# A new layout of steps in a fused two-layer Perceiver, with the context's low parts formed by POOL

## The reference, cut to what matters

```python
def _L0_xattn_ref(q, k, v, Wq, Wk, Wv, Wo):      # q = layernorm(x), k = v = ctx_1024
    qh = _split_heads(q @ Wq.T)                   # 16 heads of 16
    kh = _split_heads(k @ Wk.T)
    vh = _split_heads(v @ Wv.T)
    scores = jnp.einsum('bhqd,bhkd->bhqk', qh, kh) * scale
    attn = jax.nn.softmax(scores, axis=-1)
    out = jnp.einsum('bhqk,bhkd->bhqd', attn, vh)
    ...
    return out @ Wo.T
...
x = x + _L0_xattn_ref(_layernorm(x, axis=-1), ctx_1024, ctx_1024, ...)
x = x + _L0_attn_ref(...)     # a small attention over heads
x = x + _L0_ffn_ref(...)      # one expert of 8, picked by the largest gate
x = x + _L1_xattn_ref(...)    # as layer 0, with biases
x = x + _L1_attn_ref(...)     # a linear recurrence, gelu and a norm
x = x + _L1_ffn_ref(...)      # two of 8 experts for gate, up and down
```

## Time and profile before

| what | value |
|---|---|
| median of 3 runs | 1105.58 us (1102.05 to 1106.64) |
| the profiled execution's own time | 1103.75 us |
| its span | 1101.9 us |
| PE busy | 968.3 us (88%) |
| DVE, ACT busy | 635.1 us (58%), 557.4 us (51%) |
| POOL busy | 150.6 us (14%) |
| granted TensorE clock, mean | 0.954 of full |

### The profile page before, as it was taken

The page is one execution under the profiler, slowest core; times in us unless marked ns, Lnnn a source line. Parts: engine busy times, 40 slices in busy tenths (PEclk is TensorE's granted clock), DMA queues, the critical chain, the costliest instruction groups (busy, mean ns, idle before and its releaser), DMA issues.

```text
span 1101.9 us, 34691 instructions
## 1 busy us (share of the span) xinstructions
PE 968.3 (88%) x15092; PEld 617.5 (56%) x15092; DVE 635.1 (58%) x1063; ACT 557.4 (51%) x1028; POOL 150.6 (14%) x182
## 2 busy tenths in 40 slices
PE   4778789998989999899898898896558999999998
PEld 2455456655655665565565565665345444445887
DVE  5655655656565566666657657665457454446342
ACT  4466757565676665457456565655147212122210
POOL 4211112111111211112111121110000000000000
PEclk9989899999999999999999999998559999999999
DMA  7686465452634443343434424341101232322210
GB/s 264 185 288 192 109 203 139 115 174 70 184 101 121 106 122 86 109 104 107 109 104 117 116 73 115 86 137 42 63 1 39 77 111 81 113 79 97 96 39 20
DMA packets 70461, 123.72 MB, mean 112 GB/s; under 512 B 34420, under 2 KB 45716, under 8 KB 67048
## 3 DMA queue, kind: packets, MB, share of 16 engines
q1 hardware_dynamic: 69480, 119.84, 36.8%
q0 software_dynamic: 544, 1.34, 0.3%
q10 hardware_dynamic: 288, 0.33, 0.1%
HBM read 64.81 MB, written 17.31 MB: 75 GB/s over the span
## 4 chain that ended last, share of the span: by engine, by line
PE 67%; DVE 12%; ACT 6%; SPq 6%; issue 4%; DMA 4%; POOL 0%; ACTq 0%; DVEq 0%
PE ps L595 65%; SPq L379 6%; DVE mpart L1185 4%; ACT p L966 2%; PE ps L844 2%; DMA stage<-in_wkv 1%; DMA c32b<-in_ctxT 1%; DVE rinv L1202 1%; PE ps L730 1%; ACT ch L924 1%; DMA cl<-cparts 1%; ACT kh L941 1%; ACT k L940 1%; DMA qbscratch<-qb 1%; ACT wh L977 1%
## 5 line engine op out<-in xcount | busy, mean ns | idle before, releaser
L1185 DVE TENSOR_REDUCE mpart<-ps 128x2 f32<-128x800 f32 (+1 forms) x256 | 252.9, 990 | 132.8 <-PE ps L595 132.5
L966 ACT ACTIVATE p<-ps 128x512 f32<-128x512 f32 (+1 forms) x416 | 225.7, 600 | 80.3 <-PE ps L595 80.0
L547 POOL TENSOR_TENSOR kl<-k,kh 128x400 f16<-128x400 f32 (+1 forms) x128 | 118.9, 930 | 496.8 <-ACT kh L941 496.6
L595 PE MATMUL ps<-p,v 128*17 128x64 f32 x6656 | 138.5, 226 | 6.5 <-DVE osum L1212 6.5
L595 PE MATMUL ps<-kh,qbcur 64*128 64x400 f16 (+1 forms) x512 | 87.9, 340 | 53.9 <-DVE mpart L1185 49.6
L595 PEld LDWEIGHTS ps<-p,v 128*17 128x17 f32 x6656 | 101.9, 100 | 47.7 <-issue 32.4
L1216 DVE SCALAR_TENSOR_TENSOR wl<-w,wh 128x2048 f16<-128x2048 f32 x24 | 55.0, 2292 | 127.3 <-ACT wh L977 127.3
L595 PE MATMUL ps<-wvh,ch 128*128 128x256 f16 (+1 forms) x416 | 114.9, 276 | 0.9 <-issue 0.2
L595 PE MATMUL ps<-wvh,cl 128*128 128x256 f16 (+1 forms) x416 | 113.8, 274 | 0.4 <-issue 0.4
L595 PE MATMUL ps<-wvl,ch 128*128 128x256 f16 (+1 forms) x416 | 113.8, 274 | 0.0
L977 ACT ACTIVATE wh<-w 128x2048 f16<-128x2048 f32 x24 | 45.8, 1909 | 112.6 <-PE ps L595 112.6
(11 more groups left out here) (206 smaller groups left out, 1386.2 us busy)
## 6 DMA issues: line engine op xcount, KB each, us to landing
ks<-kh SPq DMA_DIRECT2D x256, 100.1 KB
w<-in_wgu SPq DMA_DIRECT2D x16, 1024.0 KB, 4.8
ks<-kl SPq DMA_DIRECT2D x128, 100.1 KB
w<-in_wd SPq DMA_DIRECT2D x8, 1024.0 KB, 4.7
c32a<-in_ctxT SPq DMA_DIRECT2D x16, 400.5 KB, 4.2
cparts<-ch SPq DMA_DIRECT2D x8, 800.5 KB, 6.6
cparts<-cl SPq DMA_DIRECT2D x8, 800.5 KB, 8.4
c32a<-in_ctxT SPq DMA_DIRECT2D x12, 400.0 KB, 3.2
```

Source lines behind the costliest of these rows:

```text
L547: nc.gpsimd.tensor_tensor(kl[:, mt, k0:k0 + w], k32[:, ku % 2, 0:w], kh[:, mt, k0:k0 + w], ALU.subtract).then_inc(sem("klo_done"), 1)
L595: return nc.tensor.matmul(o, lhsT, rhs, start=start, stop=stop, skip_group_check=shared)
L966: nc.scalar.activation(p32[0:n, step % PRING, BANK * side:BANK * side + BANK], ps[0:n, side, :], ACT.Exp, scale=DH ** -0.5).then_inc(sem(" ...
L1185: nc.vector.reduce_max(mpart[:, j0:j0 + 3:2, quarter], o.rearrange("p (b c) -> p b c", b=2)[:, :, 0:w], AX.X).then_inc(sem("max_done"), 1)
```

## The change

The table of units is written anew; two more tables say which tiles each `W` weighs and which units lie in the second PSUM slot. No step now has two `P` units without a `K` or `V` unit between them, the weighting is two steps behind the scores (tiles 0 and 1 both in step 3), `O` stands at the end of step 4, and `divide` half 1 at the end of step 5, `take_sums` in step 2. ACT makes the exponentials before it copies out a `K`, `N` or `V` unit that stands right before `S` (`scores_first`). In the rounds POOL forms `cl` (`ctx_low`) after the step's `kl`, where DVE did. Three stages move to other steps.

```diff
 STEP_UNITS = {0: ["V2", "S", "P0", "W"],
-              1: ["P1", "V3", "S", "P2", "W"],
...
+              4: ["K4", "S", "P5", "W", "O"],
+              5: ["V6", "P6", "K5", "S", "P7", "W"],
+              6: ["K6", "S", "P8", "W"],
...
+              10: ["N1", "S", "P13", "W"],
+              11: ["N2", "S", "P14", "W"],
+              12: ["S", "P15", "N3", "W", "T"]}
+
+WEIGH_AT = {0: (11,), 1: (12,), 3: (0, 1), **{k: (k - 2,) for k in range(4, KT)}}
+SUMS_STEP, DIVIDE_STEP = 2, 5
+
+SECOND_BANK = ("V3", "V5", "K4", "K5", "K7", "V1", "N1", "N3")
 CTX_STEPS = {4: 0, 6: 1, 8: 2, 10: 3}
-LAG = 3
...
-STAGE_AT = {(0, 4): 1, (0, 5): 2, (0, 7): 3, (0, 9): 4, (0, 12): 5, (1, 4): 6, (1, 10): 7}
+STAGE_AT = {(0, 3): 1, (0, 5): 2, (0, 7): 3, (0, 9): 4, (0, 12): 5, (1, 7): 6, (1, 12): 7}
...
+def scores_first(units):
+
+    at = units.index("S")
+    if at and units[at - 1][0] in "KNV":
+        return units[:at - 1] + ["S", units[at - 1]] + units[at + 1:]
+    return units
...
+            def ctx_low(n):
+                h, kc, u, at = n % 4 // 2, n % 2, n // 4 % 2, ctx_slot(n)
+                k0, w = HALVES[h]
+                pool.wait_ge(sem("chi_done"), n + 1)
+                nc.gpsimd.tensor_tensor(cl[u][:, kc, k0:k0 + w], c32[at][:, 0:w], ch[u][:, kc, k0:k0 + w],
+                                        ALU.subtract).then_inc(sem("clo_done"), 1)
...
                         if name[0] in "KN" and has_unit(name, g):
                             klo(round_of(name, g), int(name[1]))
+                    if k in CTX_STEPS and g + 2 < B:
+                        ctx_low(4 * (g + 2) + CTX_STEPS[k])
...
-                    for name in STEP_UNITS[k]:
+                    for name in scores_first(STEP_UNITS[k]):
                         if name == "S":
                             exps(g, k)
...
                         if name == "S":
-                            if k == LAG and g:
+                            if k == SUMS_STEP and g:
                                 take_sums(g - 1)
-                            if k == LAG + 2 and g:
-                                divide(g - 1, 1)
                         elif name != "W" and has_unit(name, g):
                             after_unit(name, round_of(name, g))
-                    if k in CTX_STEPS and g + 2 < B:
-                        split_ctx(4 * (g + 2) + CTX_STEPS[k])
+                    if k == DIVIDE_STEP and g:
+                        divide(g - 1, 1)
```

More of the change, by code:

```diff
@@ L58 @@
 STEP_UNITS = {0: ["V2", "S", "P0", "W"],
-              1: ["P1", "V3", "S", "P2", "W"],
[L60 to L64, removed]
-              7: ["K7", "S", "P9", "W"],
[L66 to L70, removed]
+              1: ["V3", "S", "P1", "W"],
+              2: ["V4", "P2", "V5", "S", "P3"],
+              3: ["W", "S", "P4"],
+              4: ["K4", "S", "P5", "W", "O"],
+              5: ["V6", "P6", "K5", "S", "P7", "W"],
+              6: ["K6", "S", "P8", "W"],
+              7: ["K7", "S", "P9", "W"],
+              8: ["V0", "P10", "V1", "S", "P11", "W"],
+              9: ["N0", "S", "P12", "W"],
+              10: ["N1", "S", "P13", "W"],
[4 more added lines that the diff above has]
+SECOND_BANK = ("V3", "V5", "K4", "K5", "K7", "V1", "N1", "N3")
 OWN_UNITS = ("V2", "V3", "V4", "V5", "V6")
 CTX_STEPS = {4: 0, 6: 1, 8: 2, 10: 3}
-LAG = 3
 PRING = 4
@@ L141, in place @@
     if name[0] in "KNV":
-        return int(name[1:]) % 2
+        return int(name[1:]) % 2 if prologue else int(name in SECOND_BANK)
     return 3 if prologue and name[0] == "P" and int(name[1:]) % 2 else 2
@@ L821, in _ @@
                             scores(g, k)
-                        elif name == "W" and k >= LAG:
-                            weigh(g, k - LAG)
+                        elif name == "W" and k > 1:
+                            for kt in WEIGH_AT[k]:
+                                weigh(g, kt)
                         elif name == "W":
-                            if g:
-                                weigh(g - 1, KT + k - LAG)
+                            for kt in WEIGH_AT[k] if g else ():
+                                weigh(g - 1, kt)
                         else:
@@ L830, in _ @@
                         event(name, layer, t)
-            for k in range(KT - LAG, KT):
-                weigh(G - 1, k)
+            for k in range(2):
+                for kt in WEIGH_AT[k]:
+                    weigh(G - 1, kt)
             run_unit("O", G - 1)
```

## The result

The changed kernel takes **1109.66 us** in the median of 20 runs (1105.68 to 1114.96), the kernel before beside it on the same chip 1104.78 us (1099.29 to 1107.93). The ratio is **1.0058**, 95% interval [1.0044, 1.0072]: slower by 0.6%, where 1097 us and faster was forecast. It is taken over all runs; the quotient of the two medians is 1.0044. The time lies between the forecast's 1077 and 1112 us, a range that took in half of the slower case, but it moved the other way. The profiled execution has a span of 1108.7 us at a granted clock of 0.948, 6.8 us more than before (1101.9).

A forecast was written before the change was run, and what follows sets the result against it. TensorE was taken as the busy engine, idling 71.6 us in rounds 0 to 14, mostly for DVE's maximum. Terms +3.2, -1.9, -1.8, -7.8, -2, +1.7, -0.3 gave -8.9 from 1103.75; median 1097 us, range 1077 to 1112.

The forecast's parts named there:

- the four groups of rounds: Rounds 0 and 1, 2 to 5, 6 and 7, 8 to 14; TensorE idle 20.2, 15.3, 4.7, 31.4 us before.
- (a) to (d): Four places where DVE isn't free, so TensorE still waits: 1.8 (a), about 0.85 (b), 0.5 (c), 4.5 us (d).
- `N2` and POOL's part: TensorE waits for POOL's `cl` before `N2` in rounds 0 to 5: 17.4 us, POOL's part 1.1 each.
- "Exponentials first": On ACT: next scores no longer wait for exponentials held up by two copies; counted in the sums, no separate size.
- copies of key units at nothing: ACT's copies end 2.4 us after the scores, the slot's next unit comes at 3.3, so no new waits.
- My 5.6 us: TensorE's idle time in each of rounds 11 and 13, with DVE kept busy by the norm and its cleaning.
- The half clock: Slow stretches at clock 0.50 in rounds 0 to 14: 6 of 8 again, -2 us, between -8 and +5.
- "I take 0 until step 7": Round 0, stage 1 one step earlier, ahead of `P5`'s maximum: DMA wait ends at the same time, 0 cost.
- DVE behind POOL: Rounds 1 and 4, step 4: `cl` meets `q_store`, 0 to 1.82 us each; half taken, 1.7 together.
- Waits for the maximum: TensorE waiting for DVE's maximum over the whole run: down from 49.6 us to 25 or less.
- The spacing itself: A key unit and `S` between two `P` put them 1.6 us apart; with DVE free no wait is left.
- the slower one: Rival: wait at `N2` at start of step 11, rounds 0 to 5, grows to 6.4 us a round; 1114 us, chance 0.18.

The follow-up runs named there:

- the 0.9953 above: The changed kernel with all low parts of the context formed by DVE instead of POOL: 1099.49 us, 0.9953 of the kernel before.
- the fastest kernel: The changed kernel with the context's last part one step earlier, stages at their steps of before, ACT in TensorE's unit order: 1075.71 us, 0.9754 of the kernel before.

## Why the prediction was wrong

**"Together -8.9", forecast; +6.8 in the profiled execution (+7.7 by the books above).** In the sum's own terms: idle time was to be 23.4, 13.4, 2.9 and 23.6 us in the four groups of rounds and was 27.2, 17.9, 2.2 and 27.4. With the delay behind POOL that is +3.1 in place of -6.6; the half clock is +6.4 in place of -2, and round 15, the tail and the prologue -1.8 in place of -0.3. The 23.6 doesn't follow from its terms: (a) to (d) with 0.3 a round, added as they stand, give 25.3. Step by step:

- **`N2` and POOL's part: right.** Forecast 3.8, 4.2, 2.2, 2.5, 2.2 and 2.5, 17.4 us; measured 4.09, 3.96, 2.04, 2.24, 2.04 and 2.24, 16.6. `cl` took 1.60 to 1.76 us (forecast 1.82), and POOL's own share is 5.1 (16.6 - 11.5; forecast 1.1 each, 6.6). The clock behind these waits belongs to a step below.
- **"Exponentials first" as a gain "in the sums", and copies of key units at nothing: the step that failed most.** Undone alone it gives 0.9902 in place of 1.0058, 17 us. I had counted the copies' end at 2.4 us after the scores against the next use of the slot at 3.3, from a step of a round in layer 0. In rounds 11 and 13 a table load of 1.28 us and `g_a` stand ahead of the exponentials, so the copies ended 4.6 us after the scores, at 594.6, and `K5` waited 1.74 us. Two more effects had no term of the order's own: 3.3 us of the waits at `N2`, which were priced with the copies behind the exponentials but put down to the layout, and 5.0 us of waits for the maximum. In the trace of before the copies of `K4` start at 585.76 in round 11 and the load only at 586.86, so the table load was there to be read, and with it what a swap would put ahead of the copies. My 5.6 us for each of rounds 11 and 13 became 8.4; with ACT in order they are 6.5 and 6.3.
- **The half clock, "-2 (between -8 and +5)": +6.4.** I had reasoned that waits which go take their slow stretches with them. Some did: those at `P7`'s 1.93 us in rounds 3 and 5 and at a wait of 4.19 in round 1. But the waits at `N2` brought four others, two of 6.8 us in rounds 0 and 1 and two of 3.4 in rounds 3 and 5; the one in round 0 at the stage grew from 6.8 to 13.7; and round 11 got one of 3.4 after a wait of 2.12. I had counted stretches (6 of 8) and not their length, which is twice or four times 3.4 us at the waits of about 4 us and more in rounds 0 and 1. The matmuls in the waits at `N2` win 8 us without a datum coming sooner.
- **"I take 0 until step 7" for the stages: wrong.** Scores of step 7 in round 0 stand at 80.3 in place of 75.5, and the stages alone are 0.6 per cent. That the wait ends at about the same time was right (69.62, before 68.99), and round 1's forecast of 12.1 us was met. But the wait grew from 5.98 to 7.41, the 1.9 us of work that had stood ahead of it now stood behind it, and was done at half clock. Idle time in round 0 was forecast at 11.3 us and is 15.1.
- **DVE behind POOL, "I take half, 1.7 together": too small as a delay, and not decisive.** The rows show 1.5 us each in rounds 1 and 4, 3.0 together, and 1.4 in round 0, which the term had left out. The Trainium skill (SBUF — State Buffer, § Who interferes with whom) has the later of the two instructions fully blocked; by that rule the term was 3.7, and the cast that ends 0.15 us after `cl`, 1.79 us instead of 0.28, agrees with it. The same section names casts among the operations that can contend, in their two-port modes, which I had left out: I had priced `ql` alone, and in rounds 1 and 4 it was the cast to `qh` that was held. That it is not decisive was shown by the kernel with the first part on DVE, 1.0058.
- **Waits for the maximum "down to 25 or less": 39.3.** Half of it is in five waits: 7.41 in round 0, `P7` 4.00 in rounds 1 and 4, 2.1 in rounds 11 and 13. The spacing itself works as told: rounds 7 and 9 have 0.3 and 0.6 us of idle time, and rounds 6 to 10, 12 and 14 gained.
- **The rival that came true** is the slower one, though not by its price. Its place was right. Its mechanism was `kl` and `cl` stretched beside DVE; they hardly were (`kl` median 0.895 us, longest 1.087; `cl` 1.60 to 1.76). The 5.0 us a round from which it was to decide was not reached: `N2` cost 2.8 us of waiting and 1.0 to 1.3 of clock. The loss came from three places at once: the half clock at `N2` (an estimated 6 to 8 us), the stages (0.6 per cent with all of them put back), and ACT's order (17 us, some of it at `N2` too). What it would have been without POOL is the 0.9953 above.

## What to carry to other kernels

When two engines' orders are separate, a change of order on one has to be followed through all its readers, in the round in which that engine is worst off, not in a typical one: a table load ahead of one instruction delays everything that is put behind it. A wait costs more than its length where TensorE's clock falls at it; test that share by filling the wait with work. Whether many short waits are better than a few long ones was not tested. Try the parts of a change alone: here one part (POOL's) gained 1.2 per cent in the old layout and lost 1.0 in the new one, and the new layout, with three single constants or lines put right, gives 2.5.

## What was not expected of the hardware

A DVE cast from f32 to f16, which has one input and took 0.28 us alone, took 1.79 us beside a POOL subtraction of 1.75, and a two-input subtraction of 0.43 us took 1.80: both ended when POOL did, 0.15 and 0.28 us after it. An instruction of eight columns, the scaling to `f_w`, took 1.47 us beside `cl` in rounds 3 and 5, and 0.29 with all low parts on DVE. The maxima, which read PSUM, stay at 0.99 us throughout, beside `cl` too. At the wait of 7.41 us the clock stood at half for 13.7 us, the last 5.1 us of the wait among them, and at the 5.98 of before for 6.8. TensorE was busy for only 7.45 of the 13.7. What stays open: why the same waits bring a slow stretch in one round and none in another (`N2` in rounds 3 and 5 does, in rounds 2 and 4 it doesn't, at 2.0 to 2.2 us), and how POOL's low parts would do against DVE's in the fastest kernel, which was not tried.
